# Zeroing a scatter table in blocks paced by the work beside it

## What is computed

```python
s = jnp.einsum('ehd,ehd->eh', q[src], k[dst]) / np.sqrt(D) + att_bias   # per edge and head
m = jax.ops.segment_max(s, src, num_segments=n)
p = jnp.exp(s - m[src])
denom = jax.ops.segment_sum(p, src, num_segments=n)
alpha = p / jnp.where(denom[src] == 0, 1.0, denom[src])
agg = jax.ops.segment_sum(alpha[:, :, None] * v[dst], src, num_segments=n)
...
x = x + _L0_gnn_ref(xn, edge_index, edge_attr_8, ...) + _L0_mix_ref(xn[None], ...)[0]
```

## Time and profile before

| | us |
|---|---|
| runs, median of 3 | 2308.97 (2303.43 to 2315.51) |
| profiled execution, its own time | 2303.62 |
| its span, first to last instruction | 2301.9 |
| GpSimd busy | 808.7 (35%) |
| TensorE busy | 2084.8 (91%) |
| Vector busy | 1312.4 (57%) |
| DMA, whole span | 176.88 MB |

### The profile page before, as it was taken

How to read it: one execution, slowest core, us unless ns; L and a number is a source line. 1 busy time by engine, 2 the same in 40 slices (tenths; PEclk the granted TensorE clock), 3 DMA queues, 4 the chain that set the end, 5 groups by cost and what they waited for, 6 DMA issues and landing times.

```text
span 2301.9 us, 31846 instructions
## 1 busy us (share of the span) xinstructions
PE 2084.8 (91%) x11907; PEld 1271.3 (55%) x11907; DVE 1312.4 (57%) x3960; ACT 713.6 (31%) x1526; POOL 808.7 (35%) x558
## 2 busy tenths in 40 slices
PE   5999876898985999998999999999999999999977
PEld 3556544443332555555775456677777754455554
DVE  5655999567981776772224544442222234279997
ACT  4211122221001554442222355554211102135552
POOL 1336888887885766760000000000000000014443
PEclk9998887899998999999999999999999999999989
...
DMA packets 104811, 176.88 MB, mean 77 GB/s; under 512 B 64513, under 2 KB 66203, under 8 KB 94698
## 3 DMA queue, kind: packets, MB, share of 16 engines
...
...
## 4 chain that ended last, share of the span: by engine, by line
PE 48%; POOL 17%; DMA 13%; DVE 10%; issue 5%; ACT 4%; SPq 2%; DVEq 0%; PEldq 0%; ACTq 0%; POOLq 0%; PEld 0%
POOL edge_table L595 16%; PE banks L203 12%; DMA edge_table<-arena 8%; PE banks L2227 6%; PE banks L2269 6%; DMA arena<-edge_table 4%; PE banks L1576 3%; PE banks L2055 2%; PE banks L2043 2%; PE banks L2030 2%; PE banks L2653 2%; PE banks L1381 2%; PE banks L1401 2%; PE banks L2079 2%; DVE arena L1294 1%
## 5 line engine op out<-in xcount | busy, mean ns | idle before, releaser
L203 PE MATMUL banks<-arena 128*125 128x512 f32 x1200 | 557.3, 612 | 16.2 <-DVE arena L2873 14.4
L595 POOL DMA_INDIRECT edge_table<-arena x313 | 492.3, 1573 | 212.9 <-DMA edge_table<-arena 116.2
L203 PEld LDWEIGHTS banks<-arena 128*125 128x125 f32 x1200 | 222.7, 194 | 266.6 <-issue 248.1
L1294 DVE TENSOR_TENSOR arena<-banks,arena 125x1000 f32<-125x1000 f32 x100 | 194.3, 1963 | 110.3 <-DMA arena<-edge_table 56.0
L2680 POOL CAST arena<-arena 125x128 f32<-125x128 uint32 x10 | 2.9, 292 | 699.2 <-DVE arena L2816 699.2
L1327 POOL TENSOR_TENSOR arena<-arena 125x1000 f32<-125x1000 f32 x90 | 206.6, 2314 | 102.8 <-DVE arena L1294 97.0
L2175 DVE SCALAR_TENSOR_TENSOR arena<-banks,arena 125x512 f32<-125x512 f32 x80 | 60.1, 751 | 189.4 <-PE banks L2269 189.4
L2227 PEld LDWEIGHTS banks<-arena 128*128 128x128 f32 x1280 | 144.0, 192 | 6.7 <-issue 6.6
L1922 DVE CUSTOM_DVE_ANT_0 arena<-banks,arena 125x512 f32<-125x512 f32 (+8 forms) x144 | 73.0, 553 | 129.0 <-PE banks L2030 126.2
L2227 PE MATMUL banks<-arena 128*128 128x125 f32 x1280 | 146.4, 276 | 0.1
L2269 PE MATMUL banks<-arena 128*125 128x512 f32 x320 | 139.2, 593 | 0.0
...
## 6 DMA issues: line engine op xcount, KB each, us to landing
...
edge_table<-arena POOLq DMA_INDIRECT x313
...
```

Source lines behind the costliest of these rows:

```text
L203: last = nc.tensor.matmul(dst, xT[:, i, :], w[:, i, 0:n], start=(i == 0), stop=(i == k - 1))
L595: pool.indirect_dma_start(d["table"], bass.IndirectOffsetOnAxis(ap=cell[0:EP, c:c + 1].bitcast(U32), axis=0), vals[0:EP, c * ROW:(c + 1) * ...
L1294: nc.vector.tensor_tensor(weights_of(m).rearrange("p (s e n) -> p s e n", s=2, e=2), unit_scores(m).rearrange("p e (s n) -> p s e n", s=2) ...
```

## The change

The blocks keep their size (2304 KB) but have 12 lines of 384 floats. `zeros` moves to a place that is free until the graph stage's keys need it. The table is zeroed in 24 pieces: two at the start as before, then 21 blocks and a tail of 128 x 12 x 328 floats by the new `zero_rest`. That function stands behind `mix_sp` in SyncE's order. It lets a piece go when TensorE has passed a step (after each of ten projection tiles, after every second output projection, after seven of the ten feed-forward tiles) and the piece before has landed. `gnn_w_sp` is called inside it, behind the tenth piece. REST no longer exists, so the mixing's weights are issued right behind the first two blocks, and Wo, W1 and W2 directly after them. Vector reduces three maxima of keys (turns 0 to 7, 8 to 19, 20 to 29) and works out how many later pieces each group needs; GpSimd waits for these counts at turns 0, 8 and 20, and for all at turn 30.

```diff
--- before.py
+++ after.py
@@ -222,8 +222,7 @@
             eng.dma_start(dst[0:EVEN], src[0:EVEN]).then_inc(s, 16)
             eng.dma_start(dst[EVEN:TP], src[EVEN:TP]).then_inc(s, 16)
 
-        ZERO_LINE, ZERO_LINES = 576, 8
-        zeros = arena[:, BIG:BIG + ZERO_LINE]
+        ZERO_LINE, ZERO_LINES = 384, 12
 
         s_table0 = sem("first_of_table_zeroed")
         s_table1 = sem("rest_of_table_zeroed")
@@ -231,7 +230,8 @@
         TURNS = EC // TC
         KEYS_AT = TOP - 4 * UP * EP
         LINES = 2 * TURNS
-        EARLY = 8
+        KEY_TURNS = (0, 8, 20, 30)
+        KEY_MAXIMA = len(KEY_TURNS) - 1
         PART_TURNS = 2
         ATT_TURN = TILES + 1
         FF_TURN = ATT_TURN + TILES
@@ -254,7 +254,9 @@
         src_i, dst_i, src_f = (early.take(EC) for _ in range(3))
         key_halves = early.take(EC).bitcast(F16).rearrange("p (b w c) -> p b w c", b=KEY_BLOCKS, w=2)
         ident16 = early.take(EP // 2).bitcast(F16)
+        MAXIMA = KEY_MAXIMA + HEADS
         hmax = early.take(48)
+        zeroed_needed = hmax[0:1, 44:44 + KEY_MAXIMA].bitcast(U32)
         rest = arena[:, 2 * SLOT:2 * SLOT + EC * ROW]
         FIRST_VALS = PART_TURNS * TC * ROW
         marks = Space(3 * SLOT, 4 * SLOT)
@@ -264,6 +266,7 @@
         keyrow = [[top_keys.take(UP * EP) for _ in range(2)] for _ in range(2)]
         keysT = marks.take(KEY_BLOCKS * EP // 2).bitcast(F16)
         key_pick = marks.take(BLOCK_KEYS // 2).bitcast(F16)
+        zeros = marks.take(ZERO_LINE)
         s_sd_in = sem("edge_ends_loaded")
         s_bias = sem("edge_bias_loaded")
         s_key = sem("keys_ready")
@@ -324,33 +327,43 @@
             spread(sp, X[0:TP, :, :].rearrange("p t c -> p (t c)"), d["x"], s_x)
 
         ZERO = EP * ZERO_LINES * ZERO_LINE
+        ZERO_ROWS = ZERO // ROW
         ZERO_PARTS = TABLE_ROWS * ROW // ZERO
-        ZERO_REST = (TABLE_ROWS * ROW - ZERO_PARTS * ZERO) // EP
-        REST_LINES = 9
-        assert EP * ZERO_REST + ZERO_PARTS * ZERO == TABLE_ROWS * ROW and ZERO_REST % REST_LINES == 0
+        TAIL_LINE = 328
+        TAIL = EP * ZERO_LINES * TAIL_LINE
+        assert ZERO == ZERO_ROWS * ROW
+        assert (CELLS + 1) * ROW <= ZERO_PARTS * ZERO + TAIL <= (CELLS + PADS + 1) * ROW
         ZERO_FIRST = 2
-        FIRST_ROWS = ZERO_FIRST * ZERO // ROW
-        ZEROED_FIRST = 16 * (ZERO_FIRST + 1)
-        ZEROED_REST = 16 * (ZERO_PARTS - ZERO_FIRST) + 1
+        LATER = ZERO_PARTS + 1 - ZERO_FIRST
+        ZEROED_FIRST = 16 * ZERO_FIRST
+        ZEROED_REST = 16 * LATER + 1
 
         def zero_part(sp, n, s):
             flat = d["table"].rearrange("r w -> (r w)")
-            sp.dma_start(flat[n * ZERO:(n + 1) * ZERO].rearrange("(p r a) -> p r a", p=EP, r=ZERO_LINES),
-                         zeros.unsqueeze(1).to_broadcast([EP, ZERO_LINES, ZERO_LINE])).then_inc(s, 16)
+            line, size = (ZERO_LINE, ZERO) if n < ZERO_PARTS else (TAIL_LINE, TAIL)
+            sp.dma_start(flat[n * ZERO:n * ZERO + size].rearrange("(p r a) -> p r a", p=EP, r=ZERO_LINES),
+                         zeros[:, 0:line].unsqueeze(1).to_broadcast([EP, ZERO_LINES, line])).then_inc(s, 16)
 
         def zero_table(sp):
 
             sp.wait_ge(s_const, 1)
-            flat = d["table"].rearrange("r w -> (r w)")
             for n in range(ZERO_FIRST):
                 zero_part(sp, n, s_table0)
-            sp.dma_start(flat[ZERO_PARTS * ZERO:TABLE_ROWS * ROW].rearrange("(p r a) -> p r a", p=EP, r=REST_LINES),
-                         zeros[:, 0:ZERO_REST // REST_LINES].unsqueeze(1)
-                         .to_broadcast([EP, REST_LINES, ZERO_REST // REST_LINES])).then_inc(s_table0, 16)
             for w, n in ((wq_m, "Wq"), (wk_m, "Wk"), (wv_m, "Wv")):
                 sp.dma_start(w.rearrange("p k n -> p (k n)"), d["L0_mix_" + n]).then_inc(s_wm, 16)
-            for n in range(ZERO_FIRST, ZERO_PARTS):
-                zero_part(sp, n, s_table1)
+
+        def zero_rest(sp):
+
+            pace = [(m_proj, 3 * n) for n in range(1, TILES + 1)]
+            pace += [(m_wo, n) for n in range(2, TILES + 1, 2)]
+            pace += [(m_f2, n) for n in (1, 2, 4, 5, 7, 8, 10)]
+            assert len(pace) == LATER
+            for i, (done, count) in enumerate(pace):
+                sp.wait_ge(done, count)
+                sp.wait_ge(s_table1, 16 * i + 1)
+                zero_part(sp, ZERO_FIRST + i, s_table1)
+                if i == TILES - 1:
+                    gnn_w_sp(sp)
 
         def table_zeroed(eng):
             eng.wait_ge(s_table0, ZEROED_FIRST)
@@ -418,22 +431,25 @@
             by_edge = vals[0:EP, :].rearrange("p (c w) -> p c w", w=ROW)
             nc.vector.memset(by_edge[:, :, HEADS:ROW], 1.0)
 
-            nc.vector.tensor_reduce(hmax[0:EP, 0:1], key[0:EP, 0:EARLY * TC], AX_X, ALU.max)
+            for i in range(KEY_MAXIMA):
+                nc.vector.tensor_reduce(hmax[0:EP, i:i + 1], key[0:EP, KEY_TURNS[i] * TC:KEY_TURNS[i + 1] * TC], AX_X, ALU.max)
             dve.wait_ge(s_bias, 16)
             by_head = bias[0:EP, 0:EC * HEADS].rearrange("p (c h) -> p h c", h=HEADS)
-            nc.vector.tensor_reduce(hmax[0:EP, 1:9], by_head, AX_X, ALU.max).then_inc(s_hstep, 1)
+            nc.vector.tensor_reduce(hmax[0:EP, KEY_MAXIMA:MAXIMA], by_head, AX_X, ALU.max).then_inc(s_hstep, 1)
             dve.wait_ge(s_hstep, 2)
-            link(dve, nc.vector.tensor_reduce(hmax[0:9, 9:10], bank(0)[0:9, 0:EP], AX_X, ALU.max))
-            nc.vector.tensor_scalar(hmax[0:9, 16:24], ident[0:9, 1:9], hmax[0:9, 9:10], None,
+            link(dve, nc.vector.tensor_reduce(hmax[0:MAXIMA, 11:12], bank(0)[0:MAXIMA, 0:EP], AX_X, ALU.max))
+            nc.vector.tensor_scalar(hmax[0:MAXIMA, 12:12 + MAXIMA], ident[0:MAXIMA, 0:MAXIMA], hmax[0:MAXIMA, 11:12], None,
                                     ALU.mult).then_inc(s_hstep, 1)
-            link(dve, nc.vector.tensor_scalar(hmax[0:1, 32:33], hmax[0:1, 9:10], float(FIRST_ROWS), float(ZEROED_REST),
-                                              ALU.is_ge, ALU.mult))
-            nc.vector.tensor_scalar(hmax[0:1, 33:34].bitcast(U32), hmax[0:1, 32:33], 1.0, None, ALU.max)
             dve.wait_ge(s_hstep, 4)
-            link(dve, nc.vector.tensor_copy(hmax[0:EP, 24:32], bank(1)[0:EP, 0:8]))
+            link(dve, nc.vector.tensor_copy(hmax[0:EP, 24:24 + MAXIMA], bank(1)[0:EP, 0:MAXIMA]))
             flat = bias[0:EP, 0:EC * HEADS].rearrange("p (c h) -> p c h", h=HEADS)
-            nc.vector.tensor_tensor(flat, flat, hmax[0:EP, 24:32].unsqueeze(1).to_broadcast([EP, EC, HEADS]),
+            nc.vector.tensor_tensor(flat, flat, hmax[0:EP, 24 + KEY_MAXIMA:24 + MAXIMA].unsqueeze(1).to_broadcast([EP, EC, HEADS]),
                                     ALU.subtract).then_inc(s_hstep, 1)
+            parts, whole = hmax[0:1, 36:36 + KEY_MAXIMA], hmax[0:1, 40:40 + KEY_MAXIMA].bitcast(U32)
+            link(dve, nc.vector.tensor_scalar(parts, hmax[0:1, 24:24 + KEY_MAXIMA], 1.0 / ZERO_ROWS, 1.0 - ZERO_FIRST,
+                                              ALU.mult, ALU.add))
+            link(dve, nc.vector.tensor_scalar(whole, parts, 0.0, float(LATER), ALU.max, ALU.min))
+            nc.vector.tensor_scalar(zeroed_needed, whole, 16.0, 1.0, ALU.mult, ALU.add).then_inc(s_hstep, 1)
 
         def rest_left(dve, w):
 
@@ -546,8 +562,9 @@
 
         def parts_pool(pool):
 
-            pool.wait_ge(s_hstep, 5)
-            need = nc.gpsimd.value_load(hmax[0:1, 33:34].bitcast(U32), min_val=1, max_val=ZEROED_REST)
+            pool.wait_ge(s_hstep, 6)
+            need = [nc.gpsimd.value_load(zeroed_needed[:, i:i + 1], min_val=1, max_val=ZEROED_REST)
+                    for i in range(KEY_MAXIMA)]
             for w in (1, 2):
                 pool.wait_ge(s_part, 2 * w - 1)
                 left = (vals, rest)[w - 1]
@@ -567,9 +584,9 @@
             for h in range(2):
                 spread_line(pe, h)
             pe.wait_ge(s_hstep, 1)
-            nc.tensor.transpose(bank(0)[0:9, 0:EP], hmax[0:EP, 0:9], ident[0:EP, 0:EP]).then_inc(s_hstep, 1)
+            nc.tensor.transpose(bank(0)[0:MAXIMA, 0:EP], hmax[0:EP, 0:MAXIMA], ident[0:EP, 0:EP]).then_inc(s_hstep, 1)
             pe.wait_ge(s_hstep, 3)
-            nc.tensor.matmul(bank(1)[0:EP, 0:8], ones[0:9, 0:EP], hmax[0:9, 16:24],
+            nc.tensor.matmul(bank(1)[0:EP, 0:MAXIMA], ones[0:MAXIMA, 0:EP], hmax[0:MAXIMA, 12:12 + MAXIMA],
                              start=True, stop=True).then_inc(s_hstep, 1)
             pe.wait_ge(s_sd_in, 48)
             for i in range(4):
@@ -582,13 +599,13 @@
         def edges_pool(pool):
             need = parts_pool(pool)
             pool.wait_ge(s_table0, ZEROED_FIRST)
-            pool.wait_ge(s_table1, need)
 
             for c in range(USED):
-                if c == EARLY * TC:
-                    pool.wait_ge(s_table1, ZEROED_REST)
                 if c % TC == 0:
                     pool.wait_ge(s_group, c // TC + 1)
+                for i, n in enumerate(KEY_TURNS):
```

(6 more changed lines are left out.)

## The result

The changed kernel takes 2328.94 us (median of six runs, 2324.53 to 2333.85) against 2308.44 for the kernel before, run on the same chip (2303.43 to 2315.51). The ratio is 1.0093 with a 95% interval of 1.0079 to 1.0107: **slower by 0.9%, 20.5 us**.

The account below looks back on a forecast made before the run. GpSimd's scatters were taken to bound the kernel until the table's handover. Zeroing at 83.4 us, minus today's 62.3, minus 5.5 for an earlier turn 1, gave +15.6 on 2308.97: 2324.6 us, range 2285 to 2343.

Parts of the forecast that it names:

- What bounds the kernel: Before the edge attention: GpSimd's row of scatters sets its start; folding work is the next bound, at most 28.3 us away.
- Price of one lone block: GpSimd's scatters beside one singly sent zeroing block: 3.8 us lost, between 3.4 and 4.6.
- the burst at 550: Three loads of 1024 KB issued near 550 us delayed scatters by 6.1 us, so 4.6 us for a block's bytes.
- some 83 us over their quiet time: Expected sign in the new profile: GpSimd's 305 columns from turn 1 on exceed their quiet time by this much.
- Edit 1: REST leaves its place before the mixing's weights: turn 1 and its first scatter come 5.5 us earlier.
- The new small steps: Vector's added reductions before the mixing, some 0.5 us, lie under TensorE's wait for weights and cost nothing.
- The volume moves behind column 8: Zeroing, some 7 blocks of it free before turn 1 today, falls on late GpSimd scatters: 83.4 us against 62.3.
- Edit 3: GpSimd's new threshold waits at turns 0, 8, 20 and 30: none should stall.
- Behind the seam: From the edge attention on: it starts as much later as the scatters end, +15.6 us, and pieces keep their length.
- (a): Rival on zeroing: delay shrinks with line length, a block costs 2.8 us, scatters end 4.7 us earlier, 2304 us; chance 0.22.
- (b): Rival on zeroing: a lone block delays only the pair at its start, 1.7 us each, 2280 us; chance 0.17.
- (c): Rival on thresholds: one comes out too high, GpSimd waits at turn 8, some +190, 2500 us; chance 0.03.

Follow-up runs that it names:

- e5: The changed kernel with pieces of a quarter of the size, four at each step, still one in flight; 2278.62 us.
- e11: As e10, but the first twenty quarter pieces are issued without waiting and turn 8 waits for these; 2274.10 us, 0.9855 of the kernel before.
- e1: The changed kernel without pace or limit: all later blocks queued behind the mixing's weights, turn 8 waits for all; 2302.54 us.
- e2: The kernel before with REST, shortened by 40 KB, moved behind all other blocks; 2299.57 us.
- e12: The kernel before with an ordinary full block where REST stood, and REST last; 2299.15 us, one run.
- e10: As e5, without the waits for the mixing's steps: quarter pieces one in flight, not paced; 2275.38 us.
- e6: The changed kernel with 24 lines of 192 floats in place of 12 of 384, same bytes and steps; 2328.83 us.
- e3: The changed kernel without the waits for the mixing's steps, whole blocks still one in flight; 2318.09 us.

## Why the prediction was right in its verdict, and what it had wrong

The forecast was 2324.6 us, +15.6, slower; it came to 2328.9, +20.5. The mechanism was the one described; two terms of the sum were off, and in part they cancelled, so that the forecast lies within 4.3 us of the median is in part luck.

- **What bounds the kernel: right.** The attention starts 24.4 us later because the last scatter is 24.1 us later. The other bound, the folding work, was met too: e5 stops at it, with the attention 30.2 us earlier and a gain of 28.9 us in the medians. The bound lies further off than that when nothing delays the graph stage: e11's folding work ends at 698.04, 10.4 us before that of the kernel before.
- **Price of one lone block: mis-sized, too low.** I took 3.8 us with 3.4 and 4.6 as ends. Take from after's excess what is no single block: the part of before's 75.4 that lies outside the zeroing (75.4-62.3 = 13.1) and the graph weights at 6.1. The remaining 90.0 us over the 20.4 blocks of the sum (an estimate, as the tail and block 2 are in it by their bytes) are **4.4 us a block**. The same reckoning gives 3.2 for two halves and 1.6 for four quarters. The wrong choice was to go by "the row of the same kind", the deep queue: the burst at 550 was the row with the same isolation, and its 4.6 us was near. The sentence "the pair it catches waits out nearly the whole transfer" was there, and should have decided. For the deep queue 3.5 us are what e1 shows, near the 3.4. Excess +33.8 instead of +21.1: 12.7 us too little. (The sign "some 83 us over their quiet time" also left out the 13.1 us that lie outside the zeroing.)
- **Edit 1, turn 1 earlier: mis-sized, too low.** 5.5 us were taken from bytes by rate; 9.7 came. e2 and e12 split it: the move frees 9.4 us at the mixing's start, of which a whole block of 2.36 MB would be 6.4, so 2.04 MB some 5.5; the bytes were reckoned rightly, and the other 3.9 are REST's own piece, which is slower than its bytes say. This gave back 4.2 us. Together 12.7-4.2 = 8.5 on the predicted +15.6 are the trace's +24.1.
- **The new small steps, cost nothing: close.** The matmuls now wait for Vector instead of the weights, 1.54 us, so the cover named is gone, but e2, with the old steps, starts only 0.9 us sooner (38.24 against 39.17). Turn 1 is not later for it.
- **The volume moves behind column 8: right in sign.** e1, with the same order and no waits, has the last scatter at 724.10; e11, which fills the free time by intent, at 693.44 against 699.61 of e10.
- **Edit 3, no stall: right.** Column 64 goes at 226.50 after 5.03 us behind a scatter's landing, a wait like those beside the other blocks; turns 20 and 30 start after 0.34 and 0.42 us.
- **Behind the seam: as said, but for the clock.** Median +20.5, seam +24.1, this execution +30.2. The last 6 us go with a lower granted clock (0.94 against 0.97 in the stretch shown above); that the median moved 3.6 us less than the seam of this one execution stays open.

**The rivals.** (a) *Shorter lines* falls: e6 halves them again and the time stays, and deep queues of lines of 2304 bytes (e2, excess 80.4) and of 1536 (e1, 82.0) cost about alike. (b) *A lone block never builds the queue* is wrong for 2304 KB; at 1.7 us a block it would be 2280. For quarters it comes true, at 1.6 us a block and 2278.6: one piece in flight is cheap when the piece lands within the slack of the two-column rule, and the size, which I had held fixed, is the point from which it decides. (c) *A wrong threshold* did not happen.

The Trainium skill's page DMA: Bandwidth & Descriptors, in the anatomy that the prediction drew on, makes a lone block 7.4 us (an estimate; the section's fit is for DMAs that GpSimd issues, where SyncE issues the blocks). The runs have 8.2 to 10.1 between e3's issues, and for a quarter 3.3 (e10) to 3.65, where the same reckoning gives 3.4. So it fits the quarter and is low for the block. A fixed part shows in the runs too: 5.0 us for a half and 3.3 for a quarter leave about 1.6 us that do not go with the bytes, an estimate. By the Trainium skill's figure a block would have cost GpSimd 4.0 us, nearer to the 4.4 than my 3.8, though still low. The Trainium skill's section on bandwidth, on the same page, also has the rule to batch transfers to 1 MiB or more for three quarters of the peak. Here the trace disagrees as a guide to time: pieces of 576 KB are slower by the byte, as the rule says (3.65 us for a quarter, 9.06 for a block) and make the kernel 50 us faster than pieces of 2304 KB, since the rate of the zeroing was never what the end waited for.
